# Attention of a fused Perceiver block on one Trainium2 core: slots taken in pairs, maxima one pair ahead, queries copied by ScalarE

## What is computed

```python
x = x + xattn(layernorm(x), ctx, ctx)      # x (4, 128, 512), ctx (4, 2048, 512), 16 heads of 32
x = x + attn(layernorm(x))                 # rms norm, projection, gated scan over 128 positions
x = x + ffn(layernorm(x))                  # 8 experts, top 2 of 8, and 2 shared ones, all 512 wide
# xattn:
scores = einsum('bthd,bshd->bhts', q * s, k * s)
w = softmax(scores, axis=-1)
out = einsum('bhts,bshd->bthd', w, v).reshape(B, T, W) @ w_proj.T + b_proj
```

## Time and profile before

| | us |
|---|---|
| median of 3 runs | 562.51 |
| lowest and highest | 559.0, 562.66 |
| the profiled execution itself | 559.89 |
| its span | 558.1 |
| TensorE busy (mean granted clock 0.978) | 491.4 |
| VectorE busy | 436.1 |
| ScalarE busy | 313.8 |
| GpSimd busy | 294.0 |

### The profile page before, as it was taken

One profiled execution on the slowest core, in us unless ns is written; L12 is line 12 of the kernel. 1 busy time (PEld: TensorE's weight loads), 2 busy tenths in 40 slices (PEclk: granted clock), 3 DMA queues, 4 the chain that ended last, 5 costly groups with the idle time before them and its releaser, 6 DMA issues.

```text
span 558.1 us, 16770 instructions
## 1 busy us (share of the span) xinstructions
PE 491.4 (88%) x6731; PEld 319.1 (57%) x6731; DVE 436.1 (78%) x667; ACT 313.8 (56%) x312; POOL 294.0 (53%) x262
## 2 busy tenths in 40 slices
PE   0669999999999999999999955969899999999993
PEld 0136556565565655565666542824587887887641
DVE  2857988888878889888892699795569999999417
ACT  3146564565565655655555372755358988888310
POOL 2347888888888878888669440484100110110050
PEclk9999999999999999999999996989899999999998
DMA  7994777777778677787598721269549999998143
GB/s 250 236 272 89 236 227 215 194 204 222 236 231 223 167 218 236 222 250 183 112 359 362 282 90 62 78 248 420 197 173 363 418 419 415 415 419 345 40 128 116
DMA packets 48222, 133.54 MB, mean 239 GB/s; under 512 B 6450, under 2 KB 31282, under 8 KB 37426
## 3 DMA queue, kind: packets, MB, share of 16 engines
q1 hardware_dynamic: 44500, 120.88, 65.6%
q0 software_dynamic: 3680, 12.06, 6.0%
HBM read 96.74 MB, written 11.01 MB: 193 GB/s over the span
## 4 chain that ended last, share of the span: by engine, by line
PE 70%; DVE 11%; POOL 6%; DMA 6%; issue 4%; ACT 1%; SPq 1%; DVEq 0%; POOLq 0%; ACTq 0%
PE bank L976 11%; PE bank L1010 11%; PE bank L995 9%; PE bank L1019 6%; PE bank L1150 5%; PE bank L1151 5%; PE bank L1152 5%; DMA kt<-in_keysT 4%; POOL xs_rows L631 3%; PE bank L1078 3%; POOL ps L588 2%; PE bank L1228 2%; PE bank L1230 2%; PE bank L1229 2%; DVE mx L682 2%
## 5 line engine op out<-in xcount | busy, mean ns | idle before, releaser
L682 DVE TENSOR_REDUCE mx<-bank 128x1 f32<-128x512 f32 x256 | 170.9, 689 | 34.7 <-PE bank L976 33.8
L459 ACT ACTIVATE pt<-bank 128x1024 f32<-128x1024 f32 x128 | 130.9, 1024 | 105.9 <-PE bank L995 105.7
L588 POOL TENSOR_TENSOR ps<-pt 128x512 f32<-128x512 f32 x128 | 162.1, 1271 | 45.3 <-ACT pt L459 43.8
L976 PE MATMUL bank<-kstk,q 96*128 96x512 f16 x256 | 103.1, 405 | 18.5 <-DVE mx L682 10.7
L777 DVE SCALAR_TENSOR_TENSOR ws<-wst,ws 128x2048 f16<-128x2048 f32 x51 | 116.8, 2311 | 2.3 <-ACT ws L482 2.1
L482 ACT ACTIVATE ws<-wst 128x2048 f16<-128x2048 f32 x48 | 90.6, 1904 | 9.3 <-PE bank L1218 5.9
L1010 PE MATMUL bank<-pt,v 128*32 128x128 f32 x2048 | 83.2, 281 | 3.9 <-ACT pt L459 3.9
L568 POOL TENSOR_TENSOR kl<-kt,kh 128x512 f16<-128x512 f32 x62 | 71.5, 1158 | 27.0 <-ACT kh L432 27.0
L1150 PE MATMUL bank<-xt,ws 128*128 128x128 f16 x480 | 81.2, 219 | 0.0
L1152 PE MATMUL bank<-xt,ws 128*128 128x128 f16 x480 | 81.2, 219 | 0.0
L1151 PE MATMUL bank<-xt,ws 128*128 128x128 f16 x480 | 81.2, 219 | 0.0
(11 more groups left out here) (161 smaller groups left out, 641.7 us busy)
## 6 DMA issues: line engine op xcount, KB each, us to landing
wst<-in_ffw SPq DMA_DIRECT2D x51, 1024.0 KB, 10.8
kt<-in_keysT SPq DMA_DIRECT2D x16, 1024.0 KB, 5.1
kstk<-kh SPq DMA_DIRECT2D x128, 128.0 KB, 2.5
v<-in_vals SPq DMA_DIRECT2D x16, 1024.0 KB, 6.8
kstk<-kl SPq DMA_DIRECT2D x64, 128.0 KB, 2.6
xs_rows<-biases SPq DMA_DIRECT2D x15, 256.0 KB, 3.4
x_tok<-xs_rows POOLq DMA_DIRECT2D x15, 256.0 KB, 8.6
ys_rows<-xn POOLq DMA_DIRECT2D x15, 256.0 KB, 6.5
```

Source lines behind the costliest of these rows:

```text
L459: act.activation(pt[:, hs % 4, :, :, :].rearrange("p j a t -> p (j a t)"), bank[:, 2 * (hs % 2):2 * (hs % 2) + 2, :].rearrange("p j n -> p ...
L588: pool.tensor_tensor(ps2[:, hs % 4, :, :], pt[:, hs % 4, 0, :, :], pt[:, hs % 4, 1, :, :], ALU.add)\
L682: dve.tensor_reduce(mx[:, a, q:q + 1], bank[:, 4 + k % 2, :], AX.X, ALU.max).then_inc(m_taken, 1)
L976: pe.matmul(bank[:, 4 + k % 2, :], q1[:, a, :], kstk[0:KS, off % 2, a, q * 512:(q + 1) * 512], start=True, stop=True).then_inc(m_ready, 1)
```

## The change

The hardware loops go; every engine's program is written out over the 16 groups, with plain numbers in the waits. A group is now four pairs of slots (p = 0 to 3), and TensorE's order in a pair is: two maxima, the scores of a slot two ahead, one maximum, the scores of the next slot, the remaining maxima, then the denominators of the two slots before and the values of this pair's two. So the f32 products of a pair stand together.

The maxima move one pair ahead: in pair 3 of group i, the first five of group i + 2 are done, and in pairs 0, 1 and 2 of group i the maxima 5 to 8, 9 to 12 and 13 to 15 of group i + 1 (MAXIMA). `q1` gets two buffers. The transposed queries no longer go through the ring of banks 4 and 5 but into the unused upper halves of banks 6 and 7, and ScalarE copies them (`take_queries`, `take_shifted`), where VectorE did. The transposes of the queries stand in pair 1, those of the shifted queries at the end of pair 2; ScalarE's copies stand behind the two exponentials of pairs 1 and 2. The splits of keys stand in pairs 0 and 1 on ScalarE, and in slots 3 and 5 on GpSimd, all for group i + 3.

SP loads keys four groups ahead and stacks them for group i + 2. At the start it loads the values of group 0 behind the keys of group 2. A wait for all denominators and an empty instruction behind it are gone (`o_ready`).

```diff
+    MAXIMA = (range(5, 9), range(9, 13), range(13, MB), range(0, 5))
+    def maxima_in(i, p):
+        j = i + 1 + p // 3
+        return [(j, k) for k in MAXIMA[p] if j < G]
+    def scores_in(i, p):
+        return [n for n in (HS * i + 2 * p + 2, HS * i + 2 * p + 3) if n < HS * G]
...
         stack(0, 1)
-        load_v(0, 0)
-        sp.wait_ge(split_lo, 2)
         stack(1, 0)
-        load_k(0, 2)
+        load_k(2)
+        load_v(0)
         stack(1, 1)
+        load_k(3)
+        for i in range(G):
+            if i + 4 < G:
+                load_k(i + 4)
+            if i + 1 < G:
+                load_v(i + 1)
+            if i + 2 < G:
+                stack(i + 2, 0)
+                stack(i + 2, 1)
...
+        def take_shifted(j):
+            act.wait_ge(sh_ready, j + 1)
+            if j >= 2:
+                act.wait_ge(st_done, HS * (j - 1))
+            act.activation(q2[:, j % 2, :, :], half_bank(6 + j % 2)[0:KM, 512:1024]
+                           .rearrange("k (a t) -> k a t", a=HG), ACT.Copy).then_inc(q2_done, 1)
...
+        for i in range(G):
+            for p in range(HS // 2):
+                for n in scores_in(i, p):
+                    exponent(n)
+                if p == 1 and i + 2 < G:
+                    take_queries(i + 2)
+                if p < 2 and i + 3 < G:
+                    split_keys(i + 3, p)
+                if p == 2 and i + 1 < G:
+                    take_shifted(i + 1)
...
+        for i in range(G):
+            for hs in range(HS):
+                pair_sum(HS * i + hs)
+                if hs in (3, 5) and i + 3 < G:
+                    for a in range(hs - 3, hs - 1):
+                        split_keys(i + 3, a)
...
+            for p in range(HS // 2):
+                for j, k in maxima_in(i, p):
+                    take_max(j, k)
+                if p == 0 and i > 0:
+                    invert(i - 1)
+                    divide(i - 1)
+                if p == 2 and i + 1 < G:
+                    shift(i + 1)
+                if p == 3 and i + 3 < G:
+                    token_queries(i + 3)
...
+                tenants = maxima_in(i, p)
+                for j, k in tenants[0:2]:
+                    max_scores(j, k)
+                for a, n in enumerate(scores_in(i, p)):
+                    scores(n)
+                    if p == 1 and a == 0 and i + 2 < G:
+                        queries(i + 2)
+                    for j, k in tenants[2 + a:3 + a]:
+                        max_scores(j, k)
+                for j, k in tenants[4:]:
+                    max_scores(j, k)
+                if i < 0:
+                    continue
+                done = [HS * i + 2 * p, HS * i + 2 * p + 1]
+                for n in (done[0] - 2, done[1] - 2):
+                    if n >= 0:
+                        denominators(n)
+                for n in done:
+                    values(n)
+                if p == 2 and i + 1 < G:
+                    shifted(i + 1)
```

418 lines of the change are left out of this document (171 added, 247 removed).

## The result

| us | before | after |
|---|---|---|
| median | 560.82 (6 runs) | 567.04 (6 runs) |
| lowest to highest | 558.87 to 562.66 | 565.4 to 569.14 |
| profiled execution (span) | 559.89 (558.1) | 569.14 (567.2) |

The ratio is 1.0115, with a 95% interval of 1.0081 to 1.0149. The forecast was 545 with a range of 534 to 557, so the miss is 22 us, on the other side of no change.

What follows compares the result with a forecast made beforehand. TensorE was taken as the bound, with VectorE and GpSimd nearly full. Groups falling from 17.0 to 15.9 us (-14.6), end -4.8 and start +4.8 sum to -14.6 from 559.89: 545 us, range 534 to 557.

Steps and rivals of the forecast that it cites:

- Pairs of slots on TensorE: TensorE's middle groups: f32 products together, a pair of four maxima takes 3.6 us, third maximum at 1.16, fourth about 1.83.
- changes of kind: TensorE switching between kinds of matmul: 0.11 us each, 26 a group before (2.9 us), 8 after (0.9 us).
- Its shift (0.6) is done before: Pair 2 of a group: VectorE's 0.6 us shift is finished in time, so the pair takes 3.6 us.
- pair 0 at 3.8: First pair of a group: VectorE, making a later group's queries (first cast 0.84), is 0.2 late, giving 3.8 us.
- Pair 1 at 3.95 for the division and pair 3 at 4.5: VectorE's inversion and division add 0.35 to pair 1; five maxima and waiting for ScalarE's shifted queries make pair 3 4.5 us.
- GpSimd hides with little to spare: GpSimd's eight sums and four subtractions take at worst 15.5 us a group, just below the group's 15.9.
- GpSimd becomes the bound: Rival, chance 0.16 shared with ScalarE: sums wait for a bank that denominators free; 16.6 us a group, 554 us.
- The start: Group 2's keys arrive at K = 32.5; ScalarE and VectorE order delays group 1's first values to 60.8, +4.8 us.
- The end: Last pairs, held by GpSimd's ten sums: 21.5 us from group 14's first values to last denominators, 4.8 less.
- What moves to ScalarE: Two query copies a group, 0.6 us each, lie in ScalarE's idle time except 0.25 us in pair 3.
- Straight code at 0: Writing out all groups instead of a hardware loop was taken to cost 0 us.
- Stacked keys late, the slower rival: Rival, chance 0.07: group i+2's stacked keys land too late for pair 3, from 5.6 us landing on; 567 us.

Runs made afterwards that it cites:

- all_fixed_unpaired3: all_fixed with the f32 products of a pair's two slots apart again on TensorE, maxima only in couples; 554.02 us, ratio 0.9868 to the kernel before.
- all_fixed: Kernel after with token queries on ScalarE and GpSimd, shift by reductions, and the start reordered on ScalarE and VectorE; 551.19 us, ratio 0.9833 to before.
- copies_back: Kernel after with ScalarE's two copies a group (queries and shifted queries) put back on VectorE; 565.09 us in one run.
- after_loop: Kernel after with TensorE's groups 2 to 13 in a hardware loop, nothing else; 565.96 us, ratio 1.0123 to the kernel before.
- all_fixed_loop: all_fixed with TensorE's groups 2 to 13 in a hardware loop of two groups; 544.52 us, ratio 0.9696 to the kernel before.

## Why the prediction was wrong, point by point

- *Pairs of slots on TensorE: right.* 3.62 for 3.6 a pair of four M, M3 and M4 within 0.03; and eight changes of kind are worth 0.90 us in a quiet group (all_fixed_unpaired3), though no gain in the medians is shown for it. TensorE's busy time fell from 15.1 to 13.8 in 16 us.
- *"Its shift (0.6) is done before" in pair 2, and pair 0 at 3.8 with VectorE's first cast at the price of the row (0.84): the step that failed.* Pair 2 took 4.21 for 3.6, and pair 0 5.03 for 3.8. The change put the token casts behind five maxima at the end of pair 3 and the shift behind the maxima of pair 2, both at moments when GpSimd is in the middle of an instruction. 0.84 in the earlier trace rows for a cast of 128 numbers was such a hold already (150.25 + 0.84 = 151.09, and a sum of GpSimd ended at 151.00): I took a wait for a duration. The trace of the kernel before had the same two casts at other lengths in other groups, here in one:

```profile
99.03 0.22 DVE L669 CAST xs<-xn 128x128 f16 x1
99.16 1.30 DVE L670 CAST xs<-xn 128x128 f16 x1
```

Together VectorE was held for 0.93 + 1.08 + 0.90 us a group beyond the 0.22, 0.22 and 0.18 of the instructions themselves; taking them away gives 15.15 in a quiet group where the kernel after has 17.10, which is 1.95 and more than the 1.1 that the forecast had the change save.
- *Pair 1 at 3.95 for the division and pair 3 at 4.5: too long.* Measured 3.63 and 4.25, and all_fixed needs 15.15 in all, so without the holds the forecast of 15.9 would have been 0.75 too cautious for a quiet group. That the mean of all_fixed, 16.08, is near 15.9 is luck: late keys and other stops take back what the sum had too much.
- *GpSimd hides with little to spare: wrong in kind.* It never made D wait in the middle, as foretold, but through the held casts its 14.6 us became part of a ring of 17.1. The rival "GpSimd becomes the bound" named the engine and a group of 16.6, but by another way (sums waiting for a bank), and it could not come out slower.
- *The start: K right, the rest K + 32.6 for K + 28.3.* Most of it is the same cause: 1.1 us up to M3, where the normalisations took 2.40 for 1.46, and 2.1 in pairs 2 and 0 behind it. Another 1.4 is TensorE's pace behind its stop, 2.3 us for the 0.9 in the sum; the prediction's other figure for it, "2 or so", was the nearer one. Pair 3 gave 0.25 back.
- *The end: 22.4 for 21.5.* Near in size, but not held as foretold: GpSimd stood for 2.96 us before its last eight sums, and TensorE had waited 1.67 us for the shift at 295.85.
- *What moves to ScalarE: right.* 0.26 in pair 3 as foretold (0.25), and no gain either (copies_back).
- *Straight code at 0: right in this kernel* (after_loop). In a faster one the loop gained 1.2% in the medians, of which the code's own part is open (all_fixed_loop).
- *Stacked keys late, the slower rival: no here.* No M waited for them in the kernel after, which is slow enough to hide them. Its mechanism is real all the same: all_fixed loses 4.9 us to it from 60 to 270 us, at landings of 5.6 us and more, as the prediction had worked out.

The Trainium skill states the rule on the page "SBUF — State Buffer", section "Who interferes with whom": VectorE and GpSimd share a pair of SBUF ports as a lock that is held for a whole instruction; a copy or cast in a two-port mode contends, an instruction with two SBUF inputs contends with a GpSimd instruction that reads SBUF, a reduction never does. The runs agree in what they can show, the times: casts of 128 numbers 1.15 to 1.30 us against 0.22 with GpSimd idle, the shift's subtraction 1.09 against 0.18, reductions at the same places 0.16 to 0.43. The ports and the mode of a cast stand in no trace. I had not weighed it; as a rival it would have been the one on the slower side.

## What to carry to other kernels

A duration in a trace is that of its surroundings: before an instruction is moved, compare its longest and shortest rows (1.30 and 0.22 for one cast in the trace before), and ask what ran beside the long ones. On this chip small casts and subtractions of VectorE between SBUF tiles should stand where GpSimd is idle, go to ScalarE, or be written as reductions; each one that meets a tensor_tensor of GpSimd costs up to that instruction's whole length, and in this kernel the rhythm of both engines then locked together. When such a bound is gone, look at the next wait by its semaphore's own DMA and not only by the name in the profile: here it was the stacked keys. The version that beats both kernels keeps the change's pairs, moves the token queries to ScalarE and GpSimd, builds the shift from reductions, and leaves TensorE's groups in a loop: 544.5 us, 3.0% below the kernel before (0.9696, interval 0.9636 to 0.9757).
